# One transformer block on one core: a new opening order, shift rows and token rounding on ScalarE, one minimum per group of maxima

## The reference

```
mod = silu(c) @ wmod                        # six vectors: sa ca ga sb cb gb
ga, gb = sign(.) * max(|.|, 0.25)
h = layernorm(x) * (1 + ca) + sa
q = (h @ Wq + bq) / sqrt(128); k = h @ Wk + bk; v = h @ Wv + bv
weights = softmax(causal(q @ k.T))          # 2048 x 2048, one head
x = x + ga * ((weights @ v) @ Wo + bo)
h = layernorm(x) * (1 + cb) + sb
mask = the 4 best of 16 blocks of 32 hidden channels, per token (router)
x = x + gb * ((relu(h @ w1.T + b1) * mask) @ w2.T + b2)
```

## Time and profile before

| | us |
|---|---|
| median of 3 runs (lowest, highest) | 113.72 (113.55, 113.88) |
| the profiled execution | 113.55 |
| its span in the profile | 111.8 |
| TensorE matmul busy | 107.3 (96%) |
| VectorE busy | 87.3 (78%) |
| ScalarE busy | 74.4 (67%) |
| GpSimd busy | 88.1 (79%) |

### The profile page before, as it was taken

The page is one execution under the profiler, slowest core; times in us unless marked ns, Lnnn a source line. Parts: engine busy times, 40 slices in busy tenths (PEclk is TensorE's granted clock), DMA queues, the critical chain, the costliest instruction groups (busy, mean ns, idle before and its releaser), DMA issues.

```text
span 111.8 us, 2013 instructions
## 1 busy us (share of the span) xinstructions
PE 107.3 (96%) x585; PEld 87.3 (78%) x585; DVE 87.3 (78%) x322; ACT 74.4 (67%) x163; POOL 88.1 (79%) x119
## 2 busy tenths in 40 slices
PE   5989999999999999999999999999999999999991
PEld 2468759878888888888888787878889888877790
DVE  5999999999999999978899379915975863874451
ACT  1337298597964299778488995998833668817710
POOL 6869877998999379999999999999995688947000
DMA  2994000000000000000000000000000000003324
GB/s 53 275 339 136 3 0 6 0 3 0 0 0 3 0 6 0 0 0 3 0 0 6 0 0 0 0 0 0 0 0 6 3 3 0 0 0 94 90 69 128
DMA packets 5879, 3.42 MB, mean 31 GB/s; under 512 B 743, under 2 KB 5483, under 8 KB 5868
## 3 DMA queue, kind: packets, MB, share of 16 engines
q1 hardware_dynamic: 5292, 3.03, 9.2%
q10 hardware_dynamic: 576, 0.26, 0.8%
HBM read 2.24 MB, written 1.05 MB: 29 GB/s over the span
## 4 chain that ended last, share of the span: by engine, by line
PE 81%; DVE 13%; issue 2%; POOL 2%
PE bank L929 14%; PE bank L930 13%; PE bank L933 13%; PE bank L1041 8%; PE bank L989 7%; PE bank L1029 6%; PE bank L1028 6%; PE bank L1073 3%; PE bank L963 2%; PE bank L1139 2%; DVE nmax L744 1%; DVE st L687 1%; PE bank L1168 1%; POOL rstd L440 1%; DVE xn L714 1%
## 5 line engine op out<-in xcount | busy, mean ns | idle before, releaser
L513 POOL TENSOR_TENSOR p_lo<-p_full,p_hi 128x512 fp32r<-128x512 f32 (+2 forms) x36 | 42.5, 1202 | 4.5 <-ACT p_full L627 4.5
L620 ACT ACTIVATE p_hi<-bank 128x512 fp32r<-128x512 f32 (+2 forms) x36 | 20.6, 571 | 6.5 <-PE bank L933 2.9
L627 ACT ACTIVATE p_full<-bank 128x512 f32<-128x512 f32 (+2 forms) x36 | 20.5, 569 | 0.6 <-POOL p_lo L513 0.6
L519 POOL TENSOR_TENSOR hid_lo<-hid_full,hid_hi 128x512 fp32r<-128x512 f32 x12 | 15.5, 1296 | 5.2 <-ACT hid_hi L656 5.2
L749 DVE TENSOR_REDUCE cmax<-bank 128x1 f32<-128x512 f32 x24 | 16.1, 685 | 1.9 <-PE bank L989 1.7
L1028 PE MATMUL bank<-g_hi,zt_hi 128*128 128x512 f32 (+3 forms) x40 | 15.2, 380 | 0.0
L1041 PE MATMUL bank<-g_lo,zt_hi 128*128 128x512 f32 (+3 forms) x40 | 14.6, 373 | 0.2 <-DVE g_lo L769 0.2
L1029 PE MATMUL bank<-g_hi,zt_lo 128*128 128x512 f32 (+3 forms) x40 | 14.5, 364 | 0.0
L929 PE MATMUL bank<-p_hi,z_hi 128*128 128x512 f32 (+2 forms) x36 | 14.0, 389 | 0.0
L989 PE MATMUL bank<-zt_hi,g_hi 128*128 128x512 f32 (+3 forms) x40 | 13.8, 386 | 0.0
L930 PE MATMUL bank<-p_hi,z_lo 128*128 128x512 f32 (+2 forms) x36 | 13.4, 373 | 0.0
(11 more groups left out here) (213 smaller groups left out, 256.0 us busy)
## 6 DMA issues: line engine op xcount, KB each, us to landing
x<-in_L_attn_y_all_dram SPq DMA_DIRECT2D x3, 256.0 KB, 3.3
out_dram<-res SPq DMA_DIRECT2D x3, 256.0 KB, 2.3
w<-in_L_ffn_w_dram SPq DMA_DIRECT2D x2, 256.0 KB, 3.9
x<-in_L_attn_y_all_dram SPq DMA_DIRECT2D x2, 128.0 KB, 2.9
wmod<-in_L_wmod_dram SPq DMA_DIRECT2D x1, 256.0 KB, 3.6
wmod<-in_L_wmod_dram ACTq DMA_DIRECT2D x1, 128.0 KB, 3.2
out_dram<-res SPq DMA_DIRECT2D x1, 128.0 KB, 1.9
wk<-in_L_attn_Wk_dram SPq DMA_DIRECT2D x1, 64.0 KB, 2.9
```

Source lines behind the costliest of these rows:

```text
L513: pool.tensor_tensor(p_lo[:, s, w:], p_full[:, n % 2, w:], p_hi[:, s, w:].bitcast(F32), ALU.subtract).then_inc(p_lo_pool, 1)
L519: pool.tensor_tensor(hid_lo[:, m, :], hid_full[:, n % 2, :], hid_hi[:, m, :].bitcast(F32), ALU.subtract).then_inc(hid_lo_pool, 1)
L620: nc.scalar.activation(p_hi[:, s, w:], src, ACT.Exp).then_inc(p_hi_s, 1)
L627: nc.scalar.activation(p_full[:, n % 2, w:], src, ACT.Exp).then_inc(p_full_s, 1)
```

## The change

It has these parts.

- **Fillers.** 32 matmuls of 128 columns instead of 8 of 512 before all work; the ten `i` words are single ones of 128 columns, eight of them between the weights and the first transposes. The first transposes (`n0`) are cut in two halves `f0` and `f1`.
- **Silu** is Identity, Tanh and Identity on ScalarE; the second column of the lift is copied by ScalarE (`z2`); `wk_t` is copied by VectorE (its new `z2`).
- **Modulation.** The second part (`z3`) goes to another bank and stands behind `q0` and `z4`.
- **Biases of Wv and Wo** are no longer matmuls. The first is an activation bias of ScalarE on one column, the second two additions of one row on GpSimd (`z13`), and `o0` waits for it. The gate row and the gated-bias row are transposes instead of full fp32 products.
- **Shift rows** of all four groups go from VectorE to ScalarE (words `b0` to `b3`), with a semaphore of their own.
- **Norm of group 1** is applied by ScalarE (`a1`) instead of VectorE (`v1`).
- **Token rounding** (`z_hi`) goes from GpSimd to ScalarE (words `u0` to `u3`); GpSimd keeps the subtraction.
- **Minimum of maxima**: one reduction for a group's four tiles behind the last one, instead of one per tile (groups 1 to 3).
- **Constants**: `future` is set whole by GpSimd, `ident_b` is cast by GpSimd, and `nmax` is cleared only where it is read.
- **New orders** of all four plans.

```diff
-WAKE = 8
+WAKE = 32
-SCALAR_NORMS = (2, 3, 4, 5, 6, 7)
+SCALAR_NORMS = (1, 2, 3, 4, 5, 6, 7)
+SHIFT_SCALAR = (0, 1, 2, 3)
 TENSOR_PLAN = """
-i1 i0 i3 z0 i2 z10 z1 n0 z2 z6 z3 q0 z4 z7 a0 a1 a2 a3 n1 p2 p1 p0 b0 q1 s0 s1 a4 a5 z5 s2 a6 s3 a7 n2 w0 a8 a9
-w1 w2 w3 a10 a11 p4 z9 p6 z8 b1 q2 o0 n3 s4 a12 p5 a13 s5 s6 a14 s7 a15 a16 w4 s8 a17 w5 a18 s9 a19 q3 a20 s10
...
+z0 z10 z1 i0 i1 i2 i3 i4 i5 i6 i7 f0 z2 i8 f1 i9 z6 q0 z4 z3 a0 a1 a2 a3 p1 n1 p0 p2 b0 q1 z7 z5 a4 s0 a5 s1
+s2 a6 a7 n2 s3 a8 p4 a9 w0 a10 w1 a11 w2 w3 p5 q2 b1 p6 z9 o0 s4 n3 s5 z8 a12 s6 a13 s7 s8 a14 a15 w4 a16 s9
...
 SCALAR_PLAN = """
-z0 z1 j0 j1 z3 z6 z11 q0 z4 n1 z9 a2 q1 e0 z5 e1 e2 n2 e3 c0 z13 z12 a3 z8 q2 e4 n3 e5 e6 e7 e8 q3 e9 e10 e11
...
+z0 z2 z1 j0 z3 j1 u0 z6 q0 z4 a1 z11 n1 a2 q1 b0 z9 z5 e0 e1 n2 e2 z13 e3 u1 a3 c0 b1 u2 q2 z12 e4 e5 z8 e6 n3
+e7 e8 e9 q3 z7 e10 u3 e11 b2 c1 e12 e13 e14 e15 e16 e17 e18 e19 a4 e20 e21 n4 e22 e23 b3 a5 e24 c2 e25 e26 e27
...
 VECTOR_PLAN = """
-j0 z0 j1 a0 z1 a1 g1 z3 u0 u1 z10 g2 v1 s0 s1 s2 s3 q0 n1 b0 g3 s4 s5 z5 s6 s7 q1 s8 s9 s10 s11 n2 b1 x0 s12 s13
...
+j0 j1 z1 a0 a1 z2 g1 u0 z3 u1 g2 z10 s0 s1 s2 q0 s3 n1 g3 q1 s4 s5 z5 s6 s7 s8 s9 n2 s10 s11 z6 x0 q2 s12 s13
...
 GPSIMD_PLAN = """
-z0 z1 z4 j0 j1 u0 p1 z7 p2 z6 z8 l0 l1 l2 p3 u1 z11 u2 l4 l5 l6 l7 l8 l9 z10 l10 l12 l13 l14 l15 l16 l17 l18 p4
...
+z0 z8 j0 j1 z1 z7 p1 p2 u0 z6 p3 l0 l1 l2 z13 u1 z4 l4 z11 l5 l6 u2 l7 l8 l9 l10 p4 l12 l13 l14 l15 l16 l17
...
@@ gpsimd
             def token_halves(g):
-                pool.wait_ge(*norm_applied(g))
-                step(pool.tensor_copy(tokens(z_hi, g), norm_rows(g)))
+                pool.wait_ge(z_hi_s, g + 1)
...
+                elif i == 13:
+                    pool.wait_ge(ga_row_s, 1)
+                    pool.wait_ge(bo_in_s, 16)
+                    step(pool.tensor_tensor(bo_gated[:], bo_row[:], ga_row[0:1, :], ALU.mult))
+                    pool.wait_ge(back_s, 1)
+                    pool.tensor_tensor(back[0:1, 0:P], back[0:1, 0:P], bo_gated[:], ALU.add).then_inc(back_bias_s, 1)
@@ scalar
-                    nc.scalar.activation(silu[:, 0:1], cols[:, C:C + 1], ACT.Exp, scale=-1.0).then_inc(exp_c_s, 1)
+                    nc.scalar.activation(silu[:, 0:1], cols[:, C:C + 1], ACT.Identity, scale=0.5)
+                    nc.scalar.activation(silu[:, 1:2], cols[:, C:C + 1], ACT.Tanh, scale=0.5).then_inc(tanh_c_s, 1)
+                    act.wait_ge(tanh_c_s, 1)
+                    nc.scalar.activation(silu[:, 2:3], silu[:, 1:2], ACT.Identity, scale=silu[:, 0:1],
+                                         bias=silu[:, 0:1]).then_inc(silu_s, 1)
...
+            def shift(g):
+                act.wait_ge(*filled(f"b{g}"))
+                act.wait_ge(q_lo_s, g + 1)
+                src = turned_bank(f"b{g}")
+                if one_turn(g):
+                    for r in range(GT):
+                        last = nc.scalar.copy(tile(g_lo, g * GT + r)[0:1, :], src[Q * r:Q * r + 1, 0:P])
+                else:
+                    last = nc.scalar.copy(grp(g_lo, g)[0:1, :], src[0:1, :])
+                last.then_inc(shift_s, 1)
+
+            def token_high(g):
+                act.wait_ge(*norm_applied(g))
+                nc.scalar.copy(tokens(z_hi, g), norm_rows(g)).then_inc(z_hi_s, 1)
@@ vector
-                dve.wait_ge(*emptied(f"a{k}"))
-                nc.vector.tensor_reduce(top, cmax[:, n, 0:g + 1], AX.X, ALU.min).then_inc(nmax_s, 1)
+                if r == GT - 1:
+                    dve.wait_ge(*emptied(f"a{k}"))
+                    tops = nmax[:, g, 0:P].rearrange("p (r o) -> p r o", r=GT)[:, :, 0]
+                    nc.vector.tensor_reduce(tops, tokens(cmax, g)[:, :, 0:g + 1], AX.X, ALU.min).then_inc(nmax_s, 1)
...
-                    dve.wait_ge(exp_c_s, 1)
-                    step(nc.vector.tensor_scalar(silu[:, 1:2], silu[:, 0:1], 1.0, None, ALU.add))
-                    step(nc.vector.reciprocal(silu[:, 2:3], silu[:, 1:2]))
-                    nc.vector.tensor_tensor(silu[:, 3:4], cols[:, C:C + 1], silu[:, 2:3], ALU.mult).then_inc(silu_s, 1)
+                elif i == 2:
+                    dve.wait_ge(wqk_mm, 2)
+                    nc.vector.tensor_copy(wk_t[:], score_bank[2][:, 0:P]).then_inc(wqk_t_s, 1)
@@ tensor
-                    mm(value_cols, wv[:], lift1[:], start=True, stop=False)
-                    mm(value_cols, bias_pad[:, BV, :], ident[:], start=False, stop=True).then_inc(wv_mm, 1)
+                    mm(value_cols, wv[:], lift1[:], start=True, stop=True).then_inc(wv_mm, 1)
...
-                    mm(back_cols, wv_t[:], wo[:], start=True, stop=False)
-                    mm(back_cols, ident[:], bias_pad[:, BO, :], start=False, stop=True)
-                    mm(gate_cols, ga_wide[:], ident[:], start=True, stop=True).then_inc(back_mm, 1)
+                    mm(back_cols, wv_t[:], wo[:], start=True, stop=True)
+                    nc.tensor.transpose(gate_cols, ga_wide[:], ident[:]).then_inc(back_mm, 1)
...
-                    mm(proj_bank[:, 0:P], gbb2_wide[:], ident[:], start=True, stop=True).then_inc(gbb2_mm, 1)
+                    nc.tensor.transpose(proj_bank[:, 0:P], gbb2_wide[:], ident[:]).then_inc(gbb2_mm, 1)
...
-                mm(ctx_bank[:, 0:GW // 2], filler[:, 0:P], filler[:, 0:GW // 2], start=True, stop=True)
+                mm(ctx_bank[:, 0:P], filler[:], filler[:], start=True, stop=True)
```

More of the change, by code:

```diff
@@ L328, in filled, with shifted_by_scalar, turn_emptied @@
             return turn_mm, turn_of[word] + k + 1
+        def shifted_by_scalar(word):
+            return word[0] == "b" and int(word[1:]) in SHIFT_SCALAR
+        def turn_emptied(n):
+            if shifted_by_scalar(turns[n]):
+                return shift_s, 1 + SHIFT_SCALAR.index(int(turns[n][1:]))
+            return turn_out, sum(not shifted_by_scalar(word) for word in turns[:n + 1])
         def emptied(word, k=0):
-            return turn_out, turn_of[word] + k + 1
+            return turn_emptied(turn_of[word] + k)
         def first_max_bank(k):
@@ L393, in _ @@
             load(wo[:], wo_in, wo_in_s)
-            load_bias(BV, bv_in, bias_vo_in_s)
-            load_bias(BO, bo_in, bias_vo_in_s)
+            load_column(BV, bv_in, bv_in_s)
+            load(bo_row[:], row(bo_in), bo_in_s)
             load_column(B2, b2_in, b2_in_s)
@@ L546, in prepare @@
                     act.wait_ge(wv_mm, 1)
-                    nc.scalar.copy(wv_t[:], value_cols).then_inc(wv_t_s, 1)
+                    act.wait_ge(bv_in_s, 16)
+                    nc.scalar.copy(wv_t[:, 1:], value_cols[:, 1:])
+                    nc.scalar.activation(wv_t[:, 0:1], value_cols[:, 0:1], ACT.Identity, bias=cols[:, BV:BV + 1]).then_inc(wv_t_s, 1)
                 elif i == 5:
@@ L912, in _ @@
             nc.vector.memset(keys[:], FURTHEST).then_inc(keys_made, 1)
-            nc.vector.memset(future[:, 0:GW - P], 0.0)
-            nc.vector.memset(nmax[:], 0.0).then_inc(ones_made, 1)
             dve.wait_ge(ident_made, 1)
@@ L959, in turn_norm, with turn_first @@
                 for i in range(GT):
[L960 to L966 removed]
+                    last = nc.tensor.transpose(tile(norm_bank, i), norm_rows(n)[:, i, :], ident[:])
+                last.then_inc(xt_mm, 1)
+            def turn_first(half):
+                if half == 0:
+                    pe.wait_ge(ident_made, 1)
+                    pe.wait_ge(ones_made, 1)
+                for i in range(2):
+                    pe.wait_ge(first_applied, 2 * half + i + 1)
+                    last = nc.tensor.transpose(tile(first_bank(half), i), norm_rows(0)[:, 2 * half + i, :], ident[:])
+                last.then_inc(xt_mm if half else first_turned, 1)
             def project_q(g):
                 if g == 0:
+                    pe.wait_ge(fold_hi_s, 1)
+                    pe.wait_ge(nt_hi_s, 1)
+                    mm(proj_bank[:], fold_hi[:], grp(zt_hi, 0), start=True, stop=False)
                     pe.wait_ge(fold_lo_s, 1)
[L971 to L972 removed]
+                    mm(proj_bank[:], fold_lo[:], grp(zt_hi, 0), start=False, stop=False)
+                    pe.wait_ge(nt_lo_s, 1)
+                    mm(proj_bank[:], fold_hi[:], grp(zt_lo, 0), start=False, stop=True).then_inc(q_mm, 1)
+                    return
+                pe.wait_ge(q_lo_s, g)
                 three(proj_bank[:], fold_hi[:], fold_lo[:], grp(zt_hi, g), grp(zt_lo, g),
@@ L1174, in prepare @@
                     pe.wait_ge(mod1_in_s, 16)
-                    for n in range(2):
-                        last = mm(score_bank[0][:, n:n + 1], tile(wmod, n), silu[:, 3:4], start=True, stop=True)
-                    last.then_inc(mod_mm, 1)
+                    for n, dst in ((CA, score_bank[0]), (SA, proj_bank)):
+                        mm(dst[:, n:n + 1], tile(wmod, n), silu[:, 2:3], start=True, stop=True).then_inc(mod_mm, 1)
                 elif i == 1:
-                    pe.wait_ge(lift_s, 1)
+                    pe.wait_ge(lift_s, 2)
```

125 lines of the change are left out of this document (56 added, 69 removed).

## The result

The changed kernel takes 114.42 us (median of 7 runs, 113.48 to 114.85), the kernel before 113.72 (median of 7, 113.55 to 114.00); the ratio is 1.0057 [1.0036, 1.0077]. It is 0.7 us slower, outside the range of 112.6 to 114.4 and on the other side of 113.7 than the 113.5 that I gave. That spread, and not a shift, is what had to be explained. In all that follows, ratios leave out single executions more than 1.5% above the fastest of their kernel; medians and counts leave out none, except where it is said.

The account below looks back on a forecast made before the run. TensorE, busy in all of 83.60 us between 25.8 and 109.4, was taken as the bound. -0.03 - 0.11 = -0.14 against the profiled 113.55 gave 113.4, taken as 113.5 since that execution was the lowest of three; range 112.6 to 114.4.

Parts of the forecast that it names:

- The fillers do not hold the clock: Rival at the opening: cold products double from 4.5 us, 0.6 covered, a few tenths beyond not; inside range, no own chance.
- up to 0.7 us: Opening fillers: later end if the clock has not risen by about 4.5 us or 128-column fillers are bound by their weights.
- The walk: New order carried engine by engine to `s4`, 25.30 instead of 25.80; chance 0.54, own range 113.0 to 114.0.
- the skipped products: Before `s4`: five TensorE instructions for Wv bias, Wo bias and gate row go, 0.55 us, already in the walk.
- -0.14: Whole kernel: -0.03 up to `s4` and -0.11 as written for the added transpose, against the profiled execution's 113.55.
- Full gain: Rival between `a3` and `s4`: most of 1.1 us of TensorE waits vanish, giving 112.6; chance 0.22.
- ScalarE late: Rival at group 1's normalisation: GpSimd's constants take 0.7 longer, delaying its power; +0.6, 114.1; chance 0.17.
- Second table load: Rival at silu: Tanh needs another table set, costing 1.2 to 1.9, so 114.6 to 115.3; chance 0.07.
- The shift rows: Shift rows moved to ScalarE: about 0.59 for 1x512 against VectorE's 0.67; by the skill's rule some tenths longer.
- all other new places of words in the dense stretch cost nothing: After `s4`: no cost while TensorE stays fed, covered by 15 to 25 us free on the other engines.
- the 0.47 of work moved over that line: At `s4`: `n3` and `z8` not yet done, `p5` already done; 0.47 given back, leaving 0.03 of gain.
- the 0.11 of the transpose: Dense stretch: the gbb2 transpose is one more TensorE instruction, costing 0.11.

Follow-up runs that it names:

- control: The changed kernel once more, without an edit; 113.91 us (113.49 to 114.83), ratio 1.0032, 5 of 12 above 114.2.
- before_short: The kernel before without the three further filler groups ahead of `z0`; 114.20 us (113.55 to 115.31), ratio 1.0040, 6 of 12 above 114.2.
- again: The changed kernel run again without an edit; 114.46 us (median of 12, 113.48 to 114.92), ratio 1.0034; its profiled execution took 113.59.
- wake48_b2v: The changed kernel with 48 fillers instead of 32 and the shift rows of group 2 back on VectorE; 114.71 us, ratio 1.0102.
- wake40: The changed kernel with 40 fillers instead of 32; 113.66 us (113.48 to 115.43), ratio 1.0000, 3 of 12 above 114.2.
- z4_behind: The changed kernel with ScalarE's `z4` (adds bv) put behind the normalisation of group 1; 113.70 us, ratio 1.0017, 2 of 12 above 114.2.
- bv_late: The changed kernel with the load of the bv column issued three queue places later; 114.51 us, ratio 1.0063, 6 of 7 above 114.2.
- wake48: The changed kernel with 48 fillers instead of 32; 114.58 us over nine executions (three far slower ones not counted), ratio 1.0057.
- wake48_order: The changed kernel with 48 fillers and, on TensorE, `a26` ahead of `s12` and `s27` ahead of `o2`; 114.44 us, ratio 1.0067.
- wake80: The changed kernel with 80 fillers instead of 32; 115.92 us (six executions, 115.16 to 116.39), ratio 1.0176.
- wake24: The changed kernel with 24 fillers instead of 32; 114.11 us (113.49 to 114.85), ratio 1.0027, 6 of 12 above 114.2.
- mid32: The changed kernel with four of the eight fillers ahead of `f0` moved right behind `z0`; 114.33 us, ratio 1.0028, 7 of 12 above 114.2.
- bv_early: The changed kernel with the load of the bv column issued earlier in its queue; 113.78 us, ratio 1.0022, 4 of 12 above 114.2.
- mid38: As `mid32`, with 38 fillers ahead of `z0` instead of 32; 113.78 us, ratio 1.0018, 2 of 12 above 114.2.
- wake40_z4: As `wake40`, with `z4` behind `a1` on ScalarE's queue; 113.85 us (113.59 to 115.45), ratio 1.0021, 4 of 12 above 114.2.

## Why the prediction was wrong

**The step that failed** is the one on the fillers and the rival "The fillers do not hold the clock". I took it that the rate is up soon after the fillers end, priced a late rise at "up to 0.7 us" of later fillers, held 0.6 of the doubling of cold products to be covered, called the rest "a few tenths" and left it "inside the range" with no chance of its own. The cover was real, but I had not asked how long a missed rise lasts. In the kernel before TensorE is fed ahead of the modulation until 5.06 us, in the changed kernel until about 4.4, and after that come a gap and four one-column products. By the rows of `control` the low rate then lasts until 9.3, not one more product or two: the cost is 1.03 us, not a few tenths. Executions above 114.2, all of which I take to be such, are 17 of the 31 of the changed kernel (5 of 7, 7 of 12, 5 of 12), against 8 of 130 of the kernel before. With more than half of the executions some 1.1 us later and the rest unmoved, the median falls at the lower end of the upper group: 114.42. The range of 112.6 to 114.4 had no case for that.

How far the median moved is luck in part. The same kernel has the medians 114.42, 114.46 and 113.91, the last of which lies inside the range; the mechanism would have been missing from the prediction all the same.

**What brought the missed rises was in the diff**, not in a price: the three wide fillers `i1 i0 i3` ahead of `z0`. I noted that the 32 fillers have as many columns as the eight of before, and dropped that before has three more behind them. `before_short` shows that taking them out is enough, with no other part of the change. That nothing else in the new opening has a share in it is not shown, and how the missing fillers lead to a missed rise in one execution and not in the next is open.

**The walk itself held**, to less than 0.5 us at every step and mostly to 0.2. By its own steps, in the profiled execution of the changed kernel and in `again`:

| step | predicted | result's profile | `again` |
|---|---|---|---|
| modulation starts | 4.5 | 4.57 | 4.65 |
| `wk_t` starts | 7.10 | 7.08 | 7.08 |
| `g_hi` starts | 10.09 | 10.10 | 9.98 |
| `a0` | 10.96 | 10.94 | 10.81 |
| last maximum ends | 14.00 | 13.68 | 13.56 |
| first last pass (`s0`) | 16.72 | 16.92 | 16.54 |
| first exp | 17.3 | 17.50 | 17.04 |
| first split | 18.65 | 18.67 | 18.29 |
| `s4` | 25.30 | 25.49 | 25.07 |

The second modulation stood before `a0` as said, the first exp came 0.9 to 1.4 us later than in the earlier trace rows without loss, and the skipped products paid for it. Where the rate rises in time, the changed kernel is nearly the kernel before: lowest times 113.48 to 113.49 against 113.54 to 113.55, and I had said -0.14.

**The rivals.** *Full gain*: did not come; TensorE's waits up to `s4` did shrink in `again` (25.07 instead of 25.30), but a part went in the dense stretch. *ScalarE late*: its place was right, its cause not. `n1` does wait for the normalisation of group 1, 0.32 in the result's profile, but because ScalarE's `z4` waits for a transfer, not because of GpSimd's constants. In `again` the column was there at about 10.3 and nothing waited; the price of bad transfers is some 0.4 us of one execution (114.05 against 113.59), and how often they come these runs don't show. *Second table load*: there is one load of 1.28 us, as before, with a Tanh behind it; the Trainium skill (ScalarE: Activation LUTs, Table sets), which lists tanh in the set of exp, agrees with the trace. *The shift rows*: the sentence of the prediction that draws on the Trainium skill (ScalarE: Activation LUTs, Rules for kernel authors) leaves out that the page gives its figure for bf16, while these rows are fp32. Here ScalarE takes 1.07 us for four of them (`again`, 37.10) and VectorE 1.18 (`wake48_b2v`, 37.44), and for the row of 1x512 ScalarE took 0.57 in the result's profile, where the walk had 0.59.

**A term mis-sized**: "all other new places of words in the dense stretch cost nothing". I had named `s12` as the gap to look for and priced it at nothing; it is there (38.31 above), about 0.2 us, and another 0.1 to 0.2 where `o2` waits for ScalarE's copy of ctx at 59.7. At `s24`, the other place that I had named, nothing waits: in `again` the shift rows end at 56.50 and the last pass starts at 56.83, right behind the one before it. The whole of the loss can be read without any reckoning of gaps. In `again` `s4` starts 0.73 earlier than before (25.07 against 25.80); less the 0.47 of work moved over that line and with the 0.11 of the transpose, TensorE should end 0.37 earlier. Its last matmul starts at 109.14 in both. So the dense stretch cost 0.37 us that I had priced at nothing, and it ate all that the opening had gained.

**Open**: why the kernel before, whose fillers at the low rate would end at the same 5.3 us as those of `wake40`, has fewer executions in the upper group (8 of 123 against 3 of 12, which chance could just give). I have no profile of one of them. Open too is why 24 fillers do as well as 32. Why the same opening showed the upper group in 2 of 12 (`z4_behind`) and 6 of 7 (`bv_late`) is open as well. Neither edit touches anything before 6 us, so I take it for chance in part, which is argued and not shown; so wide a difference would be rare by chance alone, and three of the seven times of `bv_late` may be those of a late column, as said above.

## What to carry to other kernels

Filler work ahead of the first products must be judged by many executions, not by the one that was profiled: the rate of TensorE rises at another moment in each. Count everything that keeps TensorE busy up to the first narrow products, the fillers in the order list too. An earlier start of the real work can leave some of it out, and a rise that is missed then comes microseconds later (9.3 us in `control`, 5.3 in `again`). When a median moves by 0.6% and the lowest time not at all, look at the single times before looking for a wait.

## What was unexpected of the hardware

TensorE's work began at 1.04 us (1.24 in the kernel before) and was unbroken up to the step in each of these profiles, yet the step from 1.2 to 2.4 GHz came before 3.8 us (`wake40`, `wake48`), at 4.1 (the changed kernel, result's profile), 4.8 (the kernel before), 5.5 (`wake48_order`) and 6.8 (`wake80`): from 2.7 to 5.8 us after the first filler. The Trainium skill (TensorE: Matmul & The Clock Gate, What you observe) says that this moment varies by half a microsecond either way from run to run; the spread here, 3.1 us from end to end against one, is three times as wide. The granted clock of the profile reads 1.00 through all of it, so it is not the place to see this: the length of a pair of fp32 products is, 0.39 or 0.63.

Where the step was missed, it came at 9.1 to 10.5 us (`wake24`, `mid32`, `control`, `bv_early`, `bv_late`, `mid38`, `wake40_z4`), although in these profiles TensorE had worked without a gap since the modulation began, at 4.6 to 5.3 us, and on products or fillers of 128 columns since 5.4 to 6.1.
